# Attention A of a hybrid block: the mixes of four pairs in one burst, the softmax division behind them

## The reference, cut to what matters

```python
q = x @ q_a_w.T @ q_b_w.T                 # 16 heads of 64 (pass) + 64 (rot)
ckv = x @ kv_a_w.T                        # 64 (compressed) + 64 (k_rot)
kvb = k_pass_c @ kv_b_w.T                 # per head: key 64, value 128
query = concat(q_pass, rope(q_rot)); key = concat(k_pass, rope(k_rot))
attn = softmax(query @ key.T)             # per batch and head, 256 x 256
out = (attn @ v).reshape(B, S, 16 * 128) @ o_w.T
```

## Time and profile before

| | |
|---|---|
| median of the timed runs | 1725.71 us |
| span of the profiled execution | 1723.7 us |
| PE (matmul) busy | 1647.9 us (96%) |
| DVE busy | 1192.7 us (69%) |
| ACT busy | 936.5 us (54%) |
| POOL busy | 621.5 us (36%) |
| mean granted TensorE clock | 0.987 |

### The profile page before, as it was taken

The page is one execution under the profiler, slowest core; times in us unless marked ns, Lnnn a source line. Parts: engine busy times, 40 slices in busy tenths (PEclk is TensorE's granted clock), DMA queues, the critical chain, the costliest instruction groups (busy, mean ns, idle before and its releaser), DMA issues. The chain is left out here.

```text
span 1723.7 us, 29705 instructions
## 1 busy us (share of the span) xinstructions
PE 1647.9 (96%) x9912; PEld 1378.0 (80%) x9912; DVE 1192.7 (69%) x2510; ACT 936.5 (54%) x2302; POOL 621.5 (36%) x479
## 2 busy tenths in 40 slices
PE   5699999999988999997899999999999998999998
PEld 4577777777767888886788898888889886888887
DVE  6488888888897555557576777777677678655555
ACT  3577777777754333332666676666666663333332
POOL 2555555555530000001564565565566450000000
PEclk9899999999999999998999999999999999999999
DMA  2000000000001001001000000000000000000001
GB/s 88 37 16 15 15 14 0 14 14 14 1 1 62 19 19 37 0 1 55 1 26 7 20 6 18 6 22 20 6 18 6 0 1 24 33 19 19 18 1 49
DMA packets 10628, 32.10 MB, mean 19 GB/s; under 512 B 1088, under 2 KB 5184, under 8 KB 10560
## 3 DMA queue, kind: packets, MB, share of 16 engines
q1 hardware_dynamic: 10560, 31.21, 5.3%
HBM read 29.11 MB, written 2.10 MB: 18 GB/s over the span
## 5 line engine op out<-in xcount | busy, mean ns | idle before, releaser
L381 POOL TENSOR_TENSOR ab_swapped<-ab_swapped,const 128x512 f32<-128x512 f32 x128 | 171.2, 1338 | 241.4 <-ACT ab_swapped L376 200.8
L1408 ACT ACTIVATE f_silu<-ps 128x512 f32<-128x512 f32 x128 | 76.3, 598 | 283.0 <-PE ps L117 282.9
L1518 DVE TENSOR_TENSOR f_hidden<-ps,f_silu 128x512 f32<-128x512 f32 x128 | 87.7, 690 | 202.0 <-PE ps L117 201.9
L115 PE MATMUL ps<-xh,f_wl 128*128 128x512 f32 x512 | 203.2, 397 | 1.5 <-DVE f_hidden L1518 1.5
L116 PE MATMUL ps<-xl,f_wh 128*128 128x512 f32 x512 | 202.8, 396 | 0.0
L117 PE MATMUL ps<-xh,f_wh 128*128 128x512 f32 x512 | 202.6, 396 | 0.0
L1237 POOL TENSOR_TENSOR ab_qk<-ab_qk,ab_swapped 128x512 f32<-128x512 f32 x128 | 173.5, 1355 | 10.0
L381 DVE TENSOR_TENSOR ab_qk<-ps,const 128x512 f32<-128x512 f32 x128 | 88.1, 688 | 119.6 <-PE ps L117 119.4
L704 DVE TENSOR_SCALAR aa_probs<-aa_probs,aa_inv 128x256 f32<-128x256 f32 x256 | 157.2, 656 | 4.6
L115 PE MATMUL ps<-f_wh,f_hl 128*128 128x256 f32 x512 | 144.4, 282 | 3.3 <-DVE x L1534 3.3
L1032 ACT ACTIVATE ab_probs<-ps,ab_negmax 128x128 f32<-128x128 f32 (+1 forms) x256 | 105.5, 418 | 74.9 <-DVE ab_negmax L1125 74.9
(11 more groups left out here) (189 smaller groups left out, 4842.0 us busy)
## 6 DMA issues: line engine op xcount, KB each, us to landing
f_stage<-wf_in SPq DMA_DIRECT2D x16, 768.0 KB, 4.3
b_stage<-wb_qkv_in SPq DMA_DIRECT2D x8, 768.0 KB, 4.4
a_stage<-wa_in SPq DMA_DIRECT2D x8, 608.0 KB, 3.8
x<-x_in SPq DMA_DIRECT2D x4, 512.0 KB, 7.0
bo_stage<-wb_out_in SPq DMA_DIRECT2D x8, 256.0 KB, 2.6
out<-x SPq DMA_DIRECT2D x4, 512.0 KB, 2.9
const<-const_in SPq DMA_DIRECT2D x1, 640.0 KB, 5.2
open_small_in<-small_weights SPq DMA_DIRECT2D x1, 392.0 KB, 6.8
```

The costliest lines, as they stand in the source:

```text
L115: nc.tensor.matmul(out, ll, rh, start=start, stop=False)
L381: return engine.tensor_tensor(by_batch(out), by_batch(src), table(c, rows, col), ALU.mult)
```

## The change

Only attention_a is changed.

- The division by the softmax sum leaves the probabilities: scale is gone. DVE's invert takes the reciprocal of a slot's eight sums at j = 2 and spreads each over 64 columns (wide); TensorE turns that with four transposes (turn_inverse) at j = 3, ACT copies it out (take_inverse), and DVE's normalise multiplies the mix with it, at j = 0 of the next slot, into a new SBUF tile mixed. mixed_hi and mixed_lo read that tile and no longer PSUM.
- The mixes of a slot's four pairs are issued in one burst at the end of step 3, in the order batch, key half, head, so that matmuls of the two column halves follow one another. probsT holds all four pairs of one slot. MIX has one bank, TURN two.
- Pairs go batch by batch: pair j is batch j // 2 and head j % 2. Scores of pair 0 wait for head 0's queries, those of pair 1 for head 1's.
- query_hi leaves ACT: POOL casts raw to qh inside finish_queries, between its sum and its lower part. POOL's loop is written out.

```diff
-        probsT = sb("probsT", [P, 2, 2, T])
+        probsT = sb("probsT", [P, PAIRS, 2, T])
+        wide, spread, mixed = sb("wide", [P, TG, 2, KVR]), sb("spread", [P, G]), sb("mixed", [P, G])
...
-        TURN = c.ps[:, 2, :]
+        TURN = lambda u: c.ps[:, 2 + 4 * (u % 2), :]
-        MIX = lambda s: c.ps[:, 5 + s % 2, :]
+        MIX = c.ps[:, 5, :]
+        turn_no = lambda it, s, j: (it * NG + s) * (PAIRS + 1) + j
+        batch_head = lambda j: (j // 2, j % 2)
...
             def scores(it, s, j):
-                h, b = j // 2, j % 2
+                b, h = batch_head(j)
                 if b == 0:
                     pe.wait_ge(q_lo, 2 * slot_no(it, s) + h + 1)
...
             def turn(it, s, j):
-                pe.wait_ge(scaled, g + 1)
-                after(pe, probsT_done, g)
+                pe.wait_ge(exp_done, pair_no(it, s, j) + 1)
+                after(pe, taken, u - 1)
...
+            def turn_inverse(it, s):
+                n = slot_no(it, s)
+                pe.wait_ge(wide_done, n + 1)
+                after(pe, taken, turn_no(it, s, PAIRS) - 1)
+                out = TURN(s + PAIRS)
+                for t in range(TG):
+                    ins = nc.tensor.transpose(out[:, t * P:(t + 1) * P], wide[:, t].rearrange("p h d -> p (h d)"), c.ident)
+                ins.then_inc(turned, 1)
+
+            def mix(it, s):
+                n = slot_no(it, s)
+                pe.wait_ge(taken, turn_no(it, s, PAIRS - 1) + 1)
+                after(pe, mixed_done, n)
+                for b in range(2):
+                    for k in range(2):
+                        for h in range(2):
+                            ins = nc.tensor.matmul(MIX[64 * h:64 * h + 64, b * T:(b + 1) * T], a.values[:, s * TG + b * 2 + k, :], probsT[:, 2 * b + h, k, :], start=(k == 0), stop=(k == 1))
                 ins.then_inc(pv_done, 1)
...
                 turn(it, s, j)
-                if not (first and s == 0 and j == 0):
-                    mix(*moved(it, s, j, -1))
+                if j == PAIRS - 1:
+                    turn_inverse(it, s)
...
                 if s == 1 and j == 1:
                     fold_output(it)
+                if j == PAIRS - 1:
+                    mix(it, s)
...
-            def query_hi(it, s, h):
...
             def exps(it, s, j):
+                act.wait_ge(maxed, pair_no(it, s, j) + 1)
+                if not (isinstance(n, int) and n == 0):
+                    act.wait_ge(turned, turn_no(it, s, j) - PAIRS)
+                after(act, inv_done, n - 1)
...
+            def take_inverse(it, s):
+                act.wait_ge(turned, turn_no(it, s, PAIRS) + 1)
+                after(act, mixed_done, slot_no(it, s))
+                nc.scalar.copy(spread[:], TURN(s + PAIRS)).then_inc(taken, 1)
...
-                act.wait_ge(pv_done, PAIRS * (n + 1))
+                act.wait_ge(mixed_done, n + 1)
-                nc.scalar.copy(mh[:, s % 2, :], MIX(s)).then_inc(mix_hi, 1)
+                nc.scalar.copy(mh[:, s % 2, :], mixed[:]).then_inc(mix_hi, 1)
...
-            def scale(it, s, j):
...
+            def invert(it, s):
+                dve.wait_ge(exp_done, PAIRS * (n + 1))
+                nc.vector.reciprocal(inv[:], total[:, s % 2]).then_inc(inv_done, 1)
+                dve.wait_ge(inv_done, n + 1)
+                after(dve, turned, turn_no(it, s, 0))
+                nc.vector.tensor_copy(wide[:], inv[:].unsqueeze(3).to_broadcast([P, TG, 2, KVR])).then_inc(wide_done, 1)
+
+            def normalise(it, s):
+                dve.wait_ge(pv_done, n + 1)
+                dve.wait_ge(taken, turn_no(it, s, PAIRS) + 1)
+                nc.vector.tensor_tensor(mixed[:], MIX, spread[:], ALU.mult).then_inc(mixed_done, 1)
...
                 nc.gpsimd.tensor_tensor(rows, rows, other, ALU.add).then_inc(rotated, 1)
+                pool.wait_ge(rotated, 2 * n + h + 1)
+                after(pool, scores_ready, PAIRS * (n - 2) + h + 3)
+                nc.gpsimd.tensor_copy(qh[:, s % 2, h, :], raw[:, h, :]).then_inc(q_hi, 1)
                 pool.wait_ge(q_hi, 2 * n + h + 1)
                 nc.gpsimd.tensor_tensor(ql[:, s % 2, h, :], raw[:, h, :], qh[:, s % 2, h, :].bitcast(F32), ALU.subtract).then_inc(q_lo, 1)
```

More of the change, by code:

```diff
@@ L414, in attention_a @@
         swapped = sb("swapped", [P, 2, G])
-        negmax, total, inv = (sb(n, [P, PAIRS, 2]) for n in ("negmax", "total", "inv"))
+        negmax, total, inv = sb("negmax", [P, PAIRS, 2]), sb("total", [P, 2, TG, 2]), sb("inv", [P, TG, 2])
         probs = sb("probs", [P, PAIRS, 2, T])
-        probsT = sb("probsT", [P, 2, 2, T])
+        probsT = sb("probsT", [P, PAIRS, 2, T])
+        wide, spread, mixed = sb("wide", [P, TG, 2, KVR]), sb("spread", [P, G]), sb("mixed", [P, G])
         mh, ml = sb("mh", [P, 2, G], F32R), sb("ml", [P, 2, G], F32R)
@@ L421, in attention_a @@
         proj_ready, rope_read, rotated, q_hi, q_lo = sem("proj_ready"), sem("rope_read"), sem("rotated"), sem("q_hi"), sem("q_lo")
-        scores_ready, maxed, exp_done, inv_done, scaled = sem("scores_ready"), sem("maxed"), sem("exp_done"), sem("inv_done"), sem("scaled")
-        turned, probsT_done, pv_done, mix_hi, mix_lo = sem("turned"), sem("probsT_done"), sem("pv_done"), sem("mix_hi"), sem("mix_lo")
+        scores_ready, maxed, exp_done, inv_done, wide_done, mixed_done = sem("scores_ready"), sem("maxed"), sem("exp_done"), sem("inv_done"), sem("wide_done"), sem("mixed_done")
+        turned, taken, pv_done, mix_hi, mix_lo = sem("turned"), sem("taken"), sem("pv_done"), sem("mix_hi"), sem("mix_lo")
         out_ready, out_added, swap_done, sin_done = sem("out_ready"), sem("out_added"), sem("swap_done"), sem("sin_done")
         S = lambda j: c.ps[:, j % 2, :]
-        TURN = c.ps[:, 2, :]
+        TURN = lambda u: c.ps[:, 2 + 4 * (u % 2), :]
         PROJ = lambda h: c.ps[:, 3 + h, :]
-        MIX = lambda s: c.ps[:, 5 + s % 2, :]
+        MIX = c.ps[:, 5, :]
         OUT = c.ps[:, 7, :]
@@ L496, in turn @@
             def turn(it, s, j):
-                g = pair_no(it, s, j)
-                pe.wait_ge(scaled, g + 1)
-                after(pe, probsT_done, g)
+                u = turn_no(it, s, j)
+                pe.wait_ge(exp_done, pair_no(it, s, j) + 1)
+                after(pe, taken, u - 1)
+                out = TURN(s + j)
                 for q in range(2):
                     for k in range(2):
-                        ins = nc.tensor.transpose(TURN[:, k * T + q * P:k * T + (q + 1) * P], probs[:, j, q, k * P:(k + 1) * P], c.ident)
+                        ins = nc.tensor.transpose(out[:, k * T + q * P:k * T + (q + 1) * P], probs[:, j, q, k * P:(k + 1) * P], c.ident)
                 ins.then_inc(turned, 1)
[L506 to L515, removed]
+            def turn_inverse(it, s):
[14 more added lines that the diff above has]
+                            ins = nc.tensor.matmul(MIX[64 * h:64 * h + 64, b * T:(b + 1) * T], a.values[:, s * TG + b * 2 + k, :], probsT[:, 2 * b + h, k, :], start=(k == 0), stop=(k == 1))
                 ins.then_inc(pv_done, 1)
@@ L576, in _ @@
             head_pair(HP - 1)
-            mix(*LAST)
             output(HP - 1, NG - 2, 1)
@@ L601, in swap @@
                 swap_a(nc, PROJ(h), swapped[:, h, :]).then_inc(swap_done, 1)
-            def query_hi(it, s, h):
[L604 to L608, removed]
-            def exps(it, s, j):
-                g = pair_no(it, s, j)
-                act.wait_ge(maxed, g + 1)
-                after(act, turned, g - PAIRS + 1)
+            def exps(it, s, j):
+                n, (b, h) = slot_no(it, s), batch_head(j)
+                act.wait_ge(maxed, pair_no(it, s, j) + 1)
+                if not (isinstance(n, int) and n == 0):
+                    act.wait_ge(turned, turn_no(it, s, j) - PAIRS)
+                after(act, inv_done, n - 1)
@@ L615, in exps @@
                 for q in range(2):
-                    ins = nc.scalar.activation(probs[:, j, q, :], S(j)[:, q * T:(q + 1) * T], ACT.Exp, bias=negmax[:, j, q:q + 1], accum_out=total[:, j, q:q + 1])
+                    ins = nc.scalar.activation(probs[:, j, q, :], S(j)[:, q * T:(q + 1) * T], ACT.Exp, bias=negmax[:, j, q:q + 1], accum_out=total[:, s % 2, 2 * b + q, h:h + 1])
                 ins.then_inc(exp_done, 1)
             def take_turned(it, s, j):
-                g = pair_no(it, s, j)
@@ L622, in take_turned @@
-                act.wait_ge(turned, g + 1)
-                after(act, pv_done, g - 1)
-                nc.scalar.copy(probsT[:, j % 2].rearrange("p k t -> p (k t)"), TURN).then_inc(probsT_done, 1)
+                act.wait_ge(turned, turn_no(it, s, j) + 1)
+                after(act, pv_done, slot_no(it, s))
+                nc.scalar.copy(probsT[:, j].rearrange("p k t -> p (k t)"), TURN(s + j)).then_inc(taken, 1)
+            def take_inverse(it, s):
+                act.wait_ge(turned, turn_no(it, s, PAIRS) + 1)
+                after(act, mixed_done, slot_no(it, s))
```

(22 more changed lines are left out.)

## The result

The changed kernel takes 1771.91 us (median of four, 1759.55 to 1780.38) against 1725.8: a ratio of 1.0261 (1.0223 to 1.0299), 46 us slower, where 1775 was forecast. Its runs scatter more than those of any other kernel here (21 us; before 2.5). The profiled execution has a span of 1771.3 us.

A forecast was written before the change was run, and what follows sets the result against it. TensorE was taken to bound the old kernel and a closed loop through GpSimd the changed one: 1723.7 + 27 (loop) + 22 (clock) = 1772.7 profiled, so 1775 timed; range 1752 to 1798, outer 1728 to 1815.

The forecast's parts named there:

- TensorE's saving: Attention A: burst saves 2.3 us a slot, four added transposes cost 0.44; TensorE's work falls 1.9 to about 11.5.
- step 3: TensorE's last step of a slot: scores 0.72, turn 0.44, inverses 0.44, projection 1.17, burst 2.08; 4.85 us.
- The closed loop: Attention A: next slot's head 1 queries, made on GpSimd after ScalarE's swap, hold back step 3 each slot; +27 us.
- The cast of head 1: Query cast moved to GpSimd, inside the loop's chain: taken as 0.95 us, bounds 0.10 and 1.28.
- GpSimd's start: GpSimd's chain starts behind ScalarE's swap, 4.47 us after the first scores matmul following a burst.
- a fold on ACT and DVE: Weight fold ahead of the swap, once in four slots: delays the loop by 0.9 us.
- The signs: Attention A: 2 to 3 us TensorE idle a slot, four GpSimd operations back to back, slot 14.4 us or more, clock below 1.
- The clock: TensorE falls to 1.2 GHz after its wait, on step 3: 1.4 us in one slot of two, +22 us.
- rival 3: Column halves don't overlap in plain f32 over a burst: 58 us more, 1833 us; chance 0.10.
- Rival 1: Loop holds but the clock does not fall: 1753 us, or 1742 with a 0.6 us cast; chance 0.27.
- Rival 2: GpSimd's chain ends before step 3 is reached, ScalarE closes a 12.5 us slot: 1683 us; chance 0.13.
- Rest terms: Last slot about -2, tail +0.9, start about balanced by the missing scaling; together -1 us.

The follow-up runs named there:

- e10_swap_behind_copy: Changed kernel with the old pair order, head 1's product and swap at the end of step 3, head 0's swap behind ScalarE's copy of pair 3: 1659.61 us.
- e3_fill: Changed kernel plus 8 (5 in every fourth slot) overwritten 128x512 matmuls ahead of TensorE's wait for head 1's queries: 1745.0 us.
- early swap: Changed kernel, new pair order kept, with head 1's cosine product and swap moved to the end of step 3 of the slot before: 1681.8 us.
- e11_cast_on_scalar: Changed kernel with the queries' cast back on ScalarE at its old places, head 1 in step 2 and head 0 in step 0: 1795.84 us.

## Why the prediction was right

- **TensorE's saving.** The burst was forecast at 1.98 us and measured 1.88 to the next matmul; step 3 at 4.85 and 4.82. The work left was sized too high: I forecast 11.5 us a slot without folds, and such a slot of e10_swap_behind_copy takes 253.45 - 242.57 = 10.88:

```profile
242.57 1.95 PE L527 MATMUL ps<-aa_probsT,values 128*64 128x256 f32 x16
244.44 0.38 PE L115 MATMUL ps<-kh,aa_ql 128*128 128x256 f32 x1
...
246.42 0.28 PE L115 MATMUL ps<-kh,aa_ql 128*128 128x256 f32 x1
...
253.45 1.95 PE L527 MATMUL ps<-aa_probsT,values 128*64 128x256 f32 x16
```

  A step with an output product took 202.69 - 199.52 = 3.17 us with its mix and takes 246.42 - 244.44 = 1.98 without it, so that a pair's mix cost 1.19 and not my 1.10. This has no part in the time of the changed kernel, which can't spend the saving.
- **The closed loop.** Shown three ways: undone by the order, undone by the start of the chain, and lengthened by a known dose. Its term was +27; the runs give 19 (e3_fill less before). Three sizes in it were off, and two of them cancel by luck. The cast of head 1 took 0.67 on the mean for 0.95, which is 31 x 0.28 = 9 us too much. The sum (L802) of head 1 took 1.61 in each slot instead of 1.28, 31 x 0.33 = 10 us too little: DVE's lower part of the mix (0.82), which now reads two SBUF tiles, ran beside it. I had charged that meeting to DVE and to nothing behind it; in this trace GpSimd is held too, and GpSimd is on the loop. What is left is GpSimd's start, 0.17 sooner than forecast, and a fold on ACT and DVE that puts it off by 0.57 (4.87 instead of 4.30) and not by 0.9: 4.44 on the mean for 4.70, 31 x 0.26 = 8 us too much. With 27 - 9 + 10 - 8 = 20 the terms close on the measured 19.
- **The signs.** TensorE's waits, GpSimd's four operations and the burst are as stated. The slot of 14.4 us or more is missed where the clock does not fall (14.24) and met on the mean (15.41).
- **The Trainium skill** (GPSIMD Engine Reference, Engine selection) puts one-input operations on GpSimd at about line rate. The cast's 0.64 us, half of the two-input 1.28, agrees with it, and the 0.6 that I had worked out by the page was nearer than my middle between rows.
- **The clock.** Forecast +22 (one slot in two, 1.4 us each), measured 27. The share was right, 14 of the 31 slots in the profiled execution; what a fall costs was sized too low, 1.8 us instead of 1.4, 25 us in all there. My upper bound of 2.0 us a slot did not follow from the 4.85 beside it, and three slots lost 2.6 to 2.7. So the errors of the loop and of the clock nearly cancel, and the total (49 forecast, 46 measured) is better than its terms. The outer range of 1728 to 1815 does not come out of its terms either: a cast of 0.3 without falls gives 1733, half of rival 3 on top of the forecast 1804. Rival 1, a loop without falls at 1753 (1742 with a cast of 0.6), is what e3_fill made real: 1745.
- **Rival 2** (the chain ends before step 3 is reached) is the changed kernel with the old order of pairs; the 1683 worked out for it is what that measures, 1682, with ScalarE's copy ending the slots as it says. That the early swap measures 1682 too is partly chance, as GpSimd still ends half of its slots. In the changed kernel the rival's condition, 2.4 us sooner, was not met.
- **Rival 3** fell: the halves overlap throughout.
- Rest terms (last slot, tail, start: -1) were not tested apart.

## What to carry to other kernels

Where an engine's work is shortened, look for the chain of other engines that starts behind its work and ends ahead of its next: such a loop sets the period whatever the busy shares say, and an edit that moves the point where the result is wanted by one step can turn a gain of 44 us into a loss of 46. Such a wait costs twice where TensorE's clock falls behind it, just as the critical step starts. When a wait disappears, ask which one is next; two of the three further steps here only moved it.

## What the runs showed of the hardware

- GpSimd casts a 128x512 f32 tile in 0.61 to 0.69 us, half of its two-input operation.
- Matmuls in the two 64-column halves overlap fully when issued in runs of up to four on one half, and partly in runs of eight (2.79 us instead of 1.88 for 16).
- A DVE operation with two SBUF inputs and a GpSimd operation hold each other up, and in these rows it is the later one that is held. The lower part of the mix took 0.82 us (it started at 197.11, while GpSimd's sine product ran to 197.38) instead of the 0.68 that it took in the kernel before with one input in PSUM; the sum, started beside it at 197.46, took 1.61 instead of 1.28; before attention A a DVE operation behind a running GpSimd one took 1.20 us.
- Waits of 2.2 us once a slot are followed by 1.2 GHz in some slots and not in others (2.26 at 171.11, yes; 2.25 at 186.97, no; 13 of 21 in the changed kernel, all in e11_cast_on_scalar, where TensorE also waits before step 2). With the wait filled down to less than 0.5 us the clock stayed at 1.00 from 90 to 460 us.
